# Delta memory: bf16 products that nothing reads, placed among TensorE's f32 products

## The reference, cut to what matters

```python
rk, wk = normalised heads of x, the same one token later      # 8 heads of 16
v, wk_beta = (x @ W_write.T) * beta, wk * beta                 # beta = sigmoid(x @ W_beta.T)
A = -(wkb_c @ swapaxes(wk_c, -1, -2)) * L_mask                 # chunks of 64 tokens, strictly lower
for i in range(1, 64): A[i] += A[i] @ A                        # (I - A) inverted, row by row
A = A + eye
v_c = A @ v_c; wk_cum = A @ (wkb_c * decay_exp)
def chunk_step(S, (rk_i, wk_i, v_i, wkc_i)):                   # scanned over the 8 chunks
    attn = (rk_i @ swapaxes(wk_i, -1, -2)) * L_mask, causal
    v_new = v_i - wkc_i @ S
    o_i = rk_i * decay_exp @ S + attn @ v_new
    return chunk_total * S + swapaxes(wk_i * dw, -1, -2) @ v_new, o_i
return out + o @ W_read.T
```

## Time and profile before

| | us |
|---|---|
| median of three runs (lowest, highest) | 4291.15 (4284.74, 4297.76) |
| the profiled execution | 4276.89 |
| its span, first to last instruction | 4275.1 |
| delta memory's levels, solves and chunk loop in it | 2251 to 2616 |
| mean granted clock of TensorE over the span | 0.941 |

### The profile page before, as it was taken

The page is one execution under the profiler, slowest core; times in us unless marked ns, Lnnn a source line. Parts: engine busy times, 40 slices in busy tenths (PEclk is TensorE's granted clock), DMA queues, the critical chain, the costliest instruction groups (busy, mean ns, idle before and its releaser), DMA issues. The chain is left out here.

```text
span 4275.1 us, 129071 instructions
## 1 busy us (share of the span) xinstructions
PE 3913.1 (92%) x55484; PEld 2517.2 (59%) x55484; DVE 3075.0 (72%) x3895; ACT 2135.4 (50%) x2729; POOL 2741.3 (64%) x3527
## 2 busy tenths in 40 slices
PE   8999978999999999999977876899999999999998
PEld 4333445666666666666646763566666666666664
DVE  1576167888878888888844433788888888888885
ACT  2455235556555565565631111455555555655653
POOL 0000077888878887888815222888888888888883
PEclk9899989999999999999986556999999999999998
DMA  0000010000000000000000001000000000000000
GB/s 18 1 1 1 0 70 21 12 8 32 2 28 12 7 32 2 17 2 2 2 8 4 4 4 60 2 2 22 7 12 17 13 12 7 19 10 2 2 2 11
DMA packets 14549, 52.52 MB, mean 12 GB/s; under 512 B 3856, under 2 KB 6288, under 8 KB 10768
## 3 DMA queue, kind: packets, MB, share of 16 engines
q1 hardware_dynamic: 13968, 44.13, 2.9%
HBM read 36.78 MB, written 7.34 MB: 10 GB/s over the span
## 5 line engine op out<-in xcount | busy, mean ns | idle before, releaser
L854 POOL TENSOR_TENSOR w_qk<-w_turned 128x1024 f32<-128x1024 f32 x384 | 907.3, 2363 | 31.5 <-DVE w_turned L684 29.2
L334 PEld LDWEIGHTS w_ps_y<-w_px,w_w_vo 128*128 128x128 f32 x6144 | 744.2, 192 | 112.7 <-issue 110.1
L289 PE MATMUL w_ps_qk<-w_w_qk,ZT 128*128 128x512 f32 x1536 | 761.8, 620 | 52.4 <-DVE w_turned L684 30.9
L334 PE MATMUL w_ps_y<-w_px,w_w_vo 128*128 128x128 f32 x6144 | 788.2, 277 | 2.6 <-DVE ZT L695 2.6
L885 POOL TENSOR_TENSOR w_qk<-w_qk,w_inv_norm 128x1024 f32<-128x1024 f32 x384 | 723.0, 1905 | 0.0
L548 ACT ACTIVATE w_squares<-w_ps_qk 128x1024 f32<-128x1024 f32 x384 | 392.5, 1022 | 495.6 <-PE w_ps_qk L289 494.0
L677 DVE TENSOR_TENSOR w_turned<-w_ps_qk,w_rot_l 128x1024 f32<-128x1024 f32 x384 | 469.0, 1221 | 230.7 <-ACT w_squares L548 205.6
L893 POOL TENSOR_TENSOR w_probs<-w_probs,w_row_inv 128x1024 f32<-128x1024 f32 x192 | 365.2, 1902 | 337.9 <-DVE w_row_inv L737 337.2
L289 PEld LDWEIGHTS w_ps_qk<-w_w_qk,ZT 128*128 128x128 f32 x1536 | 284.6, 197 | 350.4 <-issue 305.8
L552 ACT ACTIVATE w_px<-w_ps_w 128x1024 f32<-128x1024 f32 x384 | 378.0, 1021 | 219.0 <-PE w_ps_w L326 219.0
L688 DVE TENSOR_REDUCE w_sumsq<-w_squares 128x16 f32<-128x1024 f32 x384 | 458.6, 1194 | 1.5
(11 more groups left out here) (280 smaller groups left out, 5922.2 us busy)
## 6 DMA issues: line engine op xcount, KB each, us to landing
w_w_qk<-in_w_qk SPq DMA_DIRECT2D x12, 1024.0 KB, 4.8
kept_w_vo<-w_w_vo SPq DMA_DIRECT2D x6, 1024.0 KB, 5.1
w_w_vo<-kept_w_vo SPq DMA_DIRECT2D x6, 1024.0 KB, 4.9
w_w<-in_w SPq DMA_DIRECT2D x12, 384.0 KB, 3.1
w_w_vT<-in_w_vT SPq DMA_DIRECT2D x6, 512.0 KB, 6.3
w_w_o<-in_w_o SPq DMA_DIRECT2D x6, 512.0 KB, 7.0
w_w<-in_w SPq DMA_DIRECT2D x12, 192.0 KB, 3.1
XT<-in_x SPq DMA_DIRECT2D x1, 1024.0 KB, 4.8
```

The lines of the kernel that those rows point to most:

```text
L289: last = nc.tensor.matmul(ps_qk[:, c, :], Z[:, T.col:T.col + P], w_qk[:, T.parity, cols], start=True, stop=True)
L334: last = nc.tensor.matmul(ps_y[:, D.t * P:(D.t + 1) * P].rearrange("p (w q) -> p w q", q=WIN), w_vo[:, D.parity, h, p, :], px[:, D.odd, :, ...
L854: nc.gpsimd.tensor_tensor(qk[:, T.odd, which, :], turned[:, which, 0, :], turned[:, which, 1, :], ALU.add).then_inc(pool_add, 1)
```

## The change

A helper `fill(pair_of_banks, n)` issues n products of the bf16 identity (128x128) with a bf16 mask spread to 512 columns into the first bank of a pair; `fill_next(b, name, n)` picks the pair that the product `name` of batch b is about to write. Nothing reads what they write: the next real product starts its columns anew. They stand ahead of waits (two at a time) in the solves and levels, one between the tiles of each solve and key product, one ahead of each state or value step that is placed in W1 to T3, and two ahead of each state and value step of the last loop. No wait, no semaphore and no other instruction is changed.

```diff
-    ident = consts["ident"]
+    ident, ident_b, mask = consts["ident"], consts["ident_b"], consts["mask"]
...
+            def fill(pair_of_banks, n):
+                for _ in range(n):
+                    nc.tensor.matmul(ps[:, 2 * pair_of_banks, :], ident_b[:], spread(mask[:, 1, :], 1, [P, 512 // KEYS, KEYS]),
+                                     start=True, stop=True, skip_group_check=True)
+
+            def fill_next(b, name, n):
+                fill(ring_use(b, name) % 2, n)
...
                     for t in range(TILES):
                         for q in range(2):
                             last = gram_turned(nxt, t, q)
+                        if b is not None and t < TILES - 1:
+                            fill_next(b, "X1", 1)
                     last.then_inc(pe_g, 1)
                 if b is not None:
+                    fill_next(b, "X1", 2)
                     pe.wait_ge(dve_tt, (NL + 1) * (b + 1))
                     pe.wait_ge(dve_r, b + 1)
                     for t in range(TILES):
                         for q in range(2):
                             last = first_half(b, t, q)
+                        if t < TILES - 1:
+                            fill_next(b, "Y2", 1)
                     last.then_inc(pe_ring, 1)
...                                          (the same around gram_blocks, coupling, gram_reads, second_half)
                     if n < CHUNKS:
+                        if product not in ("W0", "T0"):
+                            fill(1 - ring_use(b, product) % 2, 1)
                         if part == 0:
                             state_step(b - 1, n)
                         else:
                             value_step(b - 1, n)
...
             def levels(b):
                 for l in range(NL):
+                    if b == 0 and l or l > 1:
+                        fill_next(b, f"W{l}", 2)
                     if l == 0:
                         pe.wait_ge(pool_t, b + 1)
...
                         between(b, f"W{l}", k)
+                    if b == 0 or l:
+                        fill_next(b, f"T{l}", 2)
                     pe.wait_ge(dve_v, NL * b + l + 1)
...
             for n in range(CHUNKS):
+                fill(ring_use(BATCH - 1, "X2") % 2, 2)
                 state_step(BATCH - 1, n)
+                fill(ring_use(BATCH - 1, "X2") % 2, 2)
                 value_step(BATCH - 1, n)
```

More of the change, by code:

```diff
@@ L1764, in solve_and_gram @@
                             last = gram_blocks(nxt, t, q)
+                        if b is not None and t < TILES - 1:
+                            fill_next(b, "Y2", 1)
                     last.then_inc(pe_g, 1)
                 if b is not None:
+                    fill_next(b, "Y2", 2)
                     pe.wait_ge(act_x1, b + 1)
@@ L1771, in solve_and_gram @@
                             last = coupling(b, t, q)
+                        if t < TILES - 1:
+                            fill_next(b, "X2", 1)
                     last.then_inc(pe_ring, 1)
@@ L1777, in solve_and_gram @@
                             last = gram_reads(nxt, t, q)
+                        if b is not None and t < TILES - 1:
+                            fill_next(b, "X2", 1)
                     last.then_inc(pe_g, 1)
                 if b is not None:
+                    fill_next(b, "X2", 2)
                     pe.wait_ge(dve_y2, 2 * b + 2)
```

## The result

The changed kernel takes 1.0055 times the kernel before (95% interval 1.0040 to 1.0069), 4306.91 against 4285.06 us as medians of 13 runs each; measured a second time the ratio was 1.0053 (1.0032 to 1.0073). So it is slower by some 22 us. The time lies in the range that was given, but the likeliest case, no measurable change, did not come (its own range ended at 4304): a slower kernel did, near the size that case B gave (+27).

The account below looks back on a forecast made before the run. TensorE sets the pace, bound by a low clock, instruction supply and waits for DVE and ACT. Terms 0.5 + 0 + 3x2.5 + 2 - 9 = +1 us, set on the 4291.15 us median, gave 4292; range 4266 to 4318.

Parts of the forecast that it names:

- the likeliest case: Whole kernel: clock high about half the time, gains and prices cancel; own range 4279 to 4304 us, chance 0.50.
- case B: Solves, levels, loop: the clock does not follow, products lie on TensorE's path at 0.43 us; +27, 4318 us, chance 0.26.
- Where the clock moves: Whole stage: the clock rises after microseconds of whole-array work; expected 0.6 to 0.8 in levels and solves, 0.9 in the loop.
- The sign that was to tell of a wrong forecast: Whole stage: forecast wrong if the mean clock stays under 0.6 or goes over 0.9.
- The loop term: Last chunk loop, output product and norm: clock rises early and stays; -9 us together, bounds -10 and +2.8.
- The -0.6 of a norm that starts warm: Norm behind the last loop's output product: starts at the high clock, saving 0.6 us, part of the loop's -9.
- The solve term: Three solves with key products: nine singles show, other products lie in waits or issue idle; +2.5 us each, bounds -1 and +5.
- The level term: Levels of batches 1 to 3: clock gain and product cost cancel; 0 us for each batch, bounds -5 and +7.
- -3 for the clock: Levels of batches 1 to 3: 3 us gained per batch, the clock being high about half the time.
- +3 for the products: Levels of batches 1 to 3: added products cost 3 us per batch on TensorE.
- Supply: Levels and solves: instruction packets come every 3.4 to 4.1 us, 131 records each on average, and limit TensorE.
- The rule that idle gaps lose the clock: Whole stage: no long idle gap between bursts, so filled waits would hold the clock; the prediction said the trace disagrees.

Follow-up runs that it names:

- the one tile: All 202 added products of the changed kernel, still 512 columns wide, on one 32x32 tile instead of the whole array; 1.0042 of the kernel before.
- the narrow products: All 202 added products of the changed kernel, each 64 columns wide instead of 512; 0.9983 of the kernel before.
- The doubled products: The changed kernel with twice the added products everywhere but in the last chunk loop (170 more); 1.0054 of the kernel before.
- the supply experiment: The kernel before with 240 very small products in the key products of each of three batches, nothing else added; 1.0037 of the kernel before.
- the solves alone: The changed kernel with only the 87 added products of the solves and key products kept; 1.0027 of the kernel before.
- the levels alone: The changed kernel with only the 83 added products of the levels kept; 0.9980 of the kernel before.
- without singles: The changed kernel without the 63 single products between the tiles of solve and key products, pairs kept; 1.0029 of the kernel before.
- levels and loop: The changed kernel without the 87 added products of the solves; 1.0010 of the kernel before.
- the loop alone: The changed kernel with only the 32 added products of the last chunk loop kept, run twice; 1.0005, then 0.9984 of the kernel before.

## Why the forecast missed and the range held

**Where the clock moves.** Right in kind. The loop rose at its start and stayed (0.96 and 0.98), as the term said. In levels and solves the forecast was "high about half the time"; a clock of 0.75 would be that, measured were 0.59 to 0.71 in the levels of batches 1 to 3 and 0.50 to 0.63 in the solves with key products. So a quarter, not a half. The sign that was to tell of a wrong forecast, a mean clock under 0.6 over the stage, did not come (0.65 and 0.69): the price of the products was off more than the clock.

**The loop term** held: -7.5 with the output product, predicted -8.4. A step came to 3.1, not 3.0. The -0.6 of a norm that starts warm is not shown: from the end of the output product to the end of the norm's products it is 12.2 us instead of 13.8, but so it is with the one tile and the narrow products too, whose loops stayed at 0.50. The term's upper bound was worked out loosely, since 0.86 us less the 0.39 of the wait is 0.47 and not 0.35; the 0.36 a step of the one-tile loop met it by luck.

**The solve term** is the first that was mis-sized, +2.5 where 5.6 was measured, half a microsecond beyond its bound. Two things were off in it. A single costs 0.54 us; the working priced 9 of them and let 9 between the key products go free in the issue idle. That idle is 7 us a batch, and 24 x 0.54 = 13 us fill it and leave 6: 18 singles and not 9 had to be charged, and the idle credited once. And the high clock, which was to shrink them, came for a tenth of the solves and not for half.

**The level term** is the second, 0 where 4.5 a batch was measured. The step that failed is "-3 for the clock" and, beside it, "+3 for the products". The one-tile kernel had these levels at 0.50 to 0.57, the clock of before, and they took 198.2 us, 5.3 more a batch: the products cost 5 and not 3. With the whole array and a clock of 0.59 to 0.71 it was 4.5 more, so the clock gave back about 1 us a batch and not 3. These are estimates, since one tile may cost less than the whole array and the levels move by 2 us a batch by themselves. Why so little comes back is in part argued. The room was taken as 5 to 7 us, from 3.5 us a packet. By records the levels of before stood at 3.8, 3.9 and 4.2 us for 128, and the solves, which wait for supply, at 3.8: an estimate from these rows leaves 2 to 3 us a batch. The doubled products agree with it, at 3.8 to 4.0 us with the clock at 0.78 to 0.88.

**Supply** held as a bound: 9 packets and 7.6 us of idle in the supply experiment. Its size was read too short, 3.4 us a packet in the solves where records give 3.8; eight packets fall into the window, but only seven times 128 records. In the changed kernel TensorE's own work took over as the bound of the solves. The Trainium skill's "mostly hidden" (Runtime: NRT & Kernel Launch, Instruction fetch mechanics) does not hold for products this short.

**The rule that idle gaps lose the clock** (the Trainium skill, TensorE: Matmul & The Clock Gate, HAM oscillation — how this bites in real kernels) would have the filled waits do it. The changed kernel's solves had 33.4 of 33.7 us busy at 0.50. Here no gap was the cause. What the added products cover is: 32 of them in the loop, at the same places, raised its clock to 0.96 and more with the whole array and 512 columns, and left it at 0.50 with one tile or with 64 columns.

**Case B** came near in size (39 less 12), and that is in part luck: it had 3 us of loss for the loop, which gained 7.5, and the singles of levels and solves were dearer than it said by nearly as much. Its condition, less than a quarter high, nearly held for levels and solves of batches 1 to 3, not for the whole stage. That the range held is luck of the same kind: the solve and level terms missed by 9 and 13 us, and the upper bound had been set by case B and not by the sum.

**Open.** Whole times and stage sums do not agree one by one. Against the mean of the two traces of before (366 us for all stages), the sums were +24 for the change and +22 measured, +20 and +16 for the supply experiment; but +25 and +11 for the solves alone, +8 and -9 for the levels alone, +7 and -7 for the narrow ones, +2 and +12 without singles, +12 and +23 for the doubled ones, +11 and +4 for levels and loop, +25 and +18 for the one tile, -1 and +2, then -5 and -7 for the loop alone. Each trace is one execution, and the unchanged part behind the stage took 1654 and 1667 us in two traces of the same kernel, so much of it is spread. The chips differ as well: the kernel before had medians of 4271, 4281 and 4279 us on the three chips of the experiments, and there is a trace of it from the last alone, beside the first one. Whether the code behind the stage, shifted by up to some hundreds of instructions, also plays a part was not tested. No version was faster than the kernel before by the 0.3% that the prediction said can be told. The levels alone and the narrow products came out 0.2% faster, with intervals that end just short of none, and with their own stages longer; the cause of that is open. The loop alone, at 0.9984 and 1.0005, is the one whose traces show where a gain would come from.

## What to carry to other kernels

Work that is added to hold a clock must lie inside a wait that lasts longer than it; put between products it is paid in full as soon as it exceeds the idle that is there, and more at the low clock (0.54 us) than at the high one (0.32). Before paying for a higher clock, ask what the stretch does at it: where a stretch that already ran high (here the first levels, 4.0 us a packet at 0.82) is no denser than a low one, the clock is not what it lacks. Count the records that a stretch works off rather than the packets that fall into it. A chain of short steps over several engines that wait for one another, like the chunk loop, is the place where a stage became shorter here (34.0 to 26.5 us), though even that did not show clearly in the whole time.

## What was not expected of the hardware

A 128x128 bf16 product of 512 columns beside small tiles costs 0.54 us alone and 0.48 in a pair at 1.2 GHz, 0.32 and 0.26 at 2.4 GHz, while 32x32 products start 0.03 us after one that holds a single tile, and 32 records of them then take 1.25 us instead of 1.0. Whether TensorE is busy does not by itself say at which clock: 33.4 of 33.7 us and 34.6 of 36.9 us busy stood at 0.50. Small products of 8 columns on one tile follow each other every 0.03 us.
